# A one-core decoder kernel: the encoder's eight row stores per four batches issued in pairs over two frames

## The reference

```python
x = _layernorm(x + attention_block(x))       # 16 heads; its own two layer norms and a ReLU feed-forward inside
x = _layernorm(x + cross_attention(x, ctx))  # 16 heads, a band of +-64 positions; call the result x3
gout = x3 @ Wg.T                             # x3 as 4096 rows, 8 experts
topv, topi = top_k(gout, 2)                  # each row goes to two experts
out = sum over the two of w * expert(x3)     # gated feed-forward of width 256
```

## Time and profile before

| | us |
|---|---|
| median of 3 runs | 1834.86 |
| the profiled execution, its own time | 1833.47 |
| its span, first to last instruction | 1831.7 |
| TensorE busy | 1330.0 (73%) |
| VectorE busy | 1176.1 (64%) |
| ScalarE busy | 774.5 (42%) |
| GpSimd busy | 543.1 (30%) |
| mean granted TensorE clock | 0.844 |

### The profile page before, as it was taken

One profiled execution on the slowest core, in us unless ns is written; L12 is line 12 of the kernel. 1 busy time (PEld: TensorE's weight loads), 2 busy tenths in 40 slices (PEclk: granted clock), 3 DMA queues, 4 the chain that ended last, 5 costly groups with the idle time before them and its releaser, 6 DMA issues. The chain is left out here.

```text
span 1831.7 us, 34467 instructions
## 1 busy us (share of the span) xinstructions
PE 1330.0 (73%) x10054; PEld 888.8 (49%) x10055; DVE 1176.1 (64%) x3540; ACT 774.5 (42%) x2050; POOL 543.1 (30%) x740
## 2 busy tenths in 40 slices
PE   4788878787878786429995888888577777545950
PEld 2455555455545454315553555555226666544740
DVE  4567768676767675348885898898481111655754
ACT  3677667676767674201221565565321111101210
POOL 1223343434243423220005555553130000341026
PEclk9799999999999998659996999999795555557975
DMA  6000000000000000012215000000100000111123
GB/s 231 14 12 13 17 21 16 24 14 24 13 24 10 18 6 17 20 38 64 64 58 190 20 21 23 20 20 4 29 23 0 0 0 0 42 52 45 56 69 94
DMA packets 83440, 65.44 MB, mean 36 GB/s; under 512 B 12016, under 2 KB 78192, under 8 KB 82416
## 3 DMA queue, kind: packets, MB, share of 16 engines
q1 hardware_dynamic: 71616, 46.06, 8.0%
q0 software_dynamic: 6656, 13.64, 2.3%
q10 hardware_dynamic: 5040, 4.11, 0.7%
HBM read 40.70 MB, written 23.07 MB: 35 GB/s over the span
## 5 line engine op out<-in xcount | busy, mean ns | idle before, releaser
L767 ACT ACTIVATE e_probs<-e_scores,e_neg_max 128x128 f32<-128x128 f32 x512 | 163.8, 400 | 91.8 <-DVE e_neg_max L971 91.7
L586 PE MATMUL e_bank_turned<-c_matrices,e_probs 128*128 128x128 f32 x1024 | 167.4, 288 | 24.6 <-ACT e_probs_t L807 21.3
L530 POOL TENSOR_TENSOR e_rstd<-e_var_eps,c_minus_half 128x1 f32<-128x1 f32 x128 | 70.5, 552 | 360.3 <-DVE e_var_eps L843 360.2
L807 ACT ACTIVATE e_probs_t<-e_bank_turned 128x512 f32<-128x512 f32 x256 | 152.4, 595 | 19.1 <-PE e_bank_turned L586 16.2
L586 PEld LDWEIGHTS e_bank_turned<-c_matrices,e_probs 128*128 128x128 f32 x1024 | 120.1, 147 | 46.0 <-issue 27.7
L763 ACT ACTIVATE e_probs<-e_scores 128x512 f32<-128x512 f32 x128 | 80.7, 630 | 116.0 <-DVE e_scores L968 115.7
L1576 ACT ACTIVATE d_probs<-d_scores 128x512 f32<-128x512 f32 x128 | 81.3, 635 | 112.1 <-DVE d_scores L1615 112.0
L1196 PE MATMUL m_wide<-up,m_rowsT 128*128 x224 | 120.3, 620 | 9.0 <-DVE m_rowsT L1249 7.3
L1793 DVE TENSOR_TENSOR n_gated<-n_gates,states 128x32 f32 x126 | 24.3, 193 | 154.1 <-ACT states L1894 154.1
L596 PE MATMUL e_bank_mix<-e_probs_t,e_values 128*32 128x128 f32 x2048 | 112.7, 293 | 4.0 <-ACT e_probs_t L807 1.3
L1855 PE MATMUL n_pz<-n_gated,n_wa 128*128 128x32 f32 x256 | 80.9, 409 | 45.3 <-DVE n_gated L1793 45.1
(11 more groups left out here) (308 smaller groups left out, 3299.3 us busy)
## 6 DMA issues: line engine op xcount, KB each, us to landing
m_rows<-scratch_sorted SPq DMA_DIRECT2D x112, 64.0 KB, 1.8
scratch_expert_out<-m_y SPq DMA_DIRECT2D x112, 64.0 KB, 1.6
e_x_in<-in_x SPq DMA_DIRECT2D x32, 64.0 KB, 1.9
e_ctx_in<-in_ctx SPq DMA_DIRECT2D x32, 64.0 KB, 2.0
up<-in_m_wgv SPq DMA_DIRECT2D x1, 2048.0 KB
up_b<-in_m_bgv SPq DMA_DIRECT2D x1, 2048.0 KB
scratch_ctxT<-e_xT_ctxT SPq DMA_DIRECT2D x32, 64.0 KB, 1.5
scratch_x<-e_x SPq DMA_DIRECT2D x32, 64.0 KB, 1.5
```

The costliest lines, as they stand in the source:

```text
L586: last = nc.tensor.transpose(turned_bank[:, j * P:(j + 1) * P], pr[k % 3][:, j, :], c["ident"][:])
L767: last = nc.scalar.activation(pr[k % 3][:, j, :], sc[k % 4][:, j, :], ACT.Exp, bias=nmax[k % 4][:, j:j + 1], scale=1.0)
L807: nc.scalar.activation(pt[k % 2][:], turned_bank[:], ACT.Copy).then_inc(probs_t_ready, 1)
```

## The change

In the encoder's GpSimd program the single call `pool_scatter` at offset 71 is replaced by four pieces, at offsets 75, 77, 83 and 85 (places 3 and 5 of the next frame, and 3 and 5 of the one after). Each issues the two stores of one of the four tiles; the first waits for the row numbers as before. `pool_scattered` goes from offset 80 to 94 (place 6 of the frame of the last pair). Within a tick the pieces stay in the order of the code, so they come behind the other GpSimd steps of their tick. The list of ticks is made 16 longer, so that the last group's steps are still within it.

```diff
-ENCODE_TICKS = range(-10, FRAME * (BATCH + SHIFT) + 48)
+ENCODE_TICKS = range(-10, FRAME * (BATCH + SHIFT) + 64)
...
-                if (n := group_at(tick, 71)) is not None:
-                    pool_scatter(nc, pool, r, c, n // SLOTS, [x3[(n - 3 + s) % 10] for s in range(SLOTS)], scr["sorted0"])
-                if (n := group_at(tick, 80)) is not None:
+                for s in range(SLOTS):
+                    if (n := group_at(tick, (75, 77, 83, 85)[s])) is not None:
+                        if s == 0:
+                            pool.wait_ge(r["rows_ready"], LEAD + n // SLOTS + 1)
+                            stand_alone(pool, c)
+                        for q in range(2):
+                            nc.gpsimd.indirect_dma_start(
+                                out=scr["sorted0"], out_offset=bass.IndirectOffsetOnAxis(ap=r["row_u"][:, s, q:q + 1], axis=0),
+                                in_=x3[(n - 3 + s) % 10][:], in_offset=None).then_inc(r["scattered"][s], 16)
+                if (n := group_at(tick, 94)) is not None:
                     pool_scattered(pool, r, n // SLOTS)
```

## The result

| | before | after |
|---|---|---|
| median, same chip | 1833.59 (1832.14 to 1838.01, 4 runs) | 1786.46 (1785.12 to 1790.21, 4 runs) |
| profiled execution, its own time | 1833.47 | 1786.06 |
| its span | 1831.7 | 1784.3 |
| mean granted TensorE clock | 0.844 | 0.862 |

The ratio is 0.9742 with the interval [0.9719, 0.9766], some 47 us faster. The forecast was 1784. Both programs have the same number of instructions. In what follows lines after the changed function have moved by seven: 987 is now 994, 933 is 940, 843 is 850, 911 is 918, 1007 is 1014; the stores are line 580.

What follows compares the result with a forecast made beforehand. Bound: in encoder frames with stores, VectorE and then TensorE wait for GpSimd's power steps behind eight stores. 36.1 + 6.5 + 6.7 = 49.3 us off 1833.47 gives 1784.2, forecast 1784 (chance 0.80); range 1777 to 1801.

Steps and rivals of the forecast that it cites:

- The stop goes, and nothing is late next: Five full encoder frames with stores become 20.11 us frames, since `placed` is hidden in a TensorE wait; 36.1 us saved.
- Sixth row: Stores at n = 23, running into attention-1-only frames: TensorE's 5.58 us gap plus about 1 us of lower clock; 6.5 saved.
- Seventh row: Stores at n = 27, from 750.54: TensorE's 6.69 us wait for x3 goes; 6.7 us saved.
- Pairs at place 3: Offsets 75 and 83, between `x2_bo` and `power(0)`: 2.8 us used of 6.0 idle on GpSimd; hidden, 3.2 to spare.
- Pairs at place 5: Offsets 77 and 85, between `by_place(1)` and `x1_b2`: `x1_b2` 1.2 us late, `power(1)` on time; cost 0.
- part of the new pairs shows: Rival: each pair at place 5 costs its 1.2 us, 17 us back in all, 1801 us; chance 0.08.
- The release: `pool_scattered` at offset 94, nine ticks behind the last pair, finds its semaphores full; cost 0.
- The tail: At the encoder's end the last two pairs land before the last `row_u` needs release, 0.8 us to spare; otherwise 2 lost.
- The shared port: Rival: VectorE and GpSimd lock shared SBUF ports, pairs hold VectorE operations; 27 us back, 1811 us; chance 0.04.
- The signs: Expected in the trace: line 987's wait gone, 20.1 us frames, no early 4 us TensorE gap, clock near 1.0.
- the stop is replaced: Rival: TensorE or the release would hold line 987 as long as GpSimd did; no change, 1833 us; chance 0.03.
- the pairs lie on the path: Rival: GpSimd steps behind each pair set the frame, 11 us per group for 7.2 lost; 1861 us; chance 0.05.

Runs made afterwards that it cites:

- warm_stop: Kernel before with its eight-store stops, twenty extra matmuls filling TensorE's gap in six of them; 1825.28 us, ratio 0.9929.
- fours_place3: Changed kernel with four stores at offset 75 and four at 83, both place 3; 1790.83 us, ratio 0.9779.
- one_block_place3_b: Changed kernel with all eight stores in one piece at offset 75 (place 3), repeated on the third chip; 1804.58 us, ratio 0.9813.
- fours_75_77: Changed kernel with four stores at offset 75 (place 3) and four at 77 (place 5), in one frame; 1788.86 us, ratio 0.9732.
- release_only: Kernel before, eight stores still at offset 71, only pool_scattered moved from 80 to 94 and the tick list lengthened; 1837.32 us, ratio 0.9988.
- fours_71_75_b: Changed kernel with four stores at offset 71 (place 7) and four at 75 (place 3), repeated on the third chip; 1793.69 us, ratio 0.9758.
- one_block_place5: Changed kernel with all eight stores in one piece at offset 77 (place 5); 1826.73 us, ratio 0.997.
- fours_71_75: Changed kernel with four stores at offset 71 (place 7) and four at 75 (place 3), on the first chip; 1803.7 us, ratio 0.9806.
- one_block_place3: Changed kernel with all eight stores in one piece at offset 75 (place 3), on the first chip; 1823.8 us, ratio 0.9916.

## Why the prediction was right

Point by point, by its own steps:

- **The stop goes, and nothing is late next.** Right. All frames from 243.15 to 589.13 are 20.1 to 20.2 us but the four with `picked` (21.0 to 21.4). 345.98 us against 381.54: 35.6 saved, 36.1 predicted. What is missing are two frames of 20.2 and one with `picked` of 21.4, where I had counted 20.11 and 21.0; the kernel before has frames of 20.19 and 21.34 too.
- **Sixth row.** From the fifth stop's end to the `power(1)` behind the sixth row: 710.06 - 620.86 = 89.20 before, 672.05 - 589.13 = 82.92 after. 6.3 saved, 6.5 predicted. The sum was right, its parts hardly: I wrote a gap of 5.6 and 1 us of clock, and `warm_stop` passes the same stretch in 87.14 us, so about 2.1 of it is the clock and 4.2 the wait. That the two errors cancel is luck.
- **Seventh row.** From the moment at which VectorE has written the variance for `power(3)` of batch 30 to the start of that of batch 31: 766.31 - 751.75 = 14.56 before, 721.53 - 713.58 = 7.95 after. 6.6 saved, 6.7 predicted. The 4 us that I took for it at the lower end of the range stand nowhere in the working.
- **Eighth row.** 0 predicted. 35.6 + 6.3 + 6.6 = 48.5 of the 48.4 us between the two ends, so nothing is left for it.
- **Pairs at place 3.** 3.2 us to spare predicted, 3.11 left. That it is slack and not chance shows where it is used up: four stores there cost nothing in the frames (`fours_place3`), eight cost 1.4 to 2.9 us in two frames (`one_block_place3_b`), where 10.1 us of issues go into 6.0 us of idle time and 2.2 come out as a wait.
- **Pairs at place 5.** `x1_b2` 1.2 us late predicted, 0.9 measured; `power(1)` on time. The rival *part of the new pairs shows* is out by those frames, and `fours_75_77` shows that even twice the piece stays hidden but for 0.2 us.
- **The release.** Cost 0: by `release_only`, ratio 0.9988.
- **The tail.** The seventh group's last store ends at 727.18 and `row_u` is written at 729.45, behind a wait of 0.17 us for VectorE's own `keep_rows`; the release does not hold it. I had put 2.0 us between the two points; it is 2.3.
- **The shared port.** The rule of the Trainium skill (SBUF — State Buffer, in "SBUF: two separate sides") that I set against the rows of the stores took no time here either: beside the second pair line 975 takes 0.67 us, within its usual 0.63 to 0.69, and the stores keep their 0.96. I had put the rule too widely: the page says that descriptors starve beside VectorE's modes that use both ports, not beside every operation with two inputs, and line 933, on whose row I leaned, has two inputs. The trace has a nearer test in the very operation that is stretched elsewhere, line 994 at 714.25 and 722.13 of the changed kernel: a store starts 0.2 us before each of them ends, and they take 0.35 us, as against 0.34 at 700.43 with no store beside. What agrees with the lock are VectorE's operations beside GpSimd's arithmetic: line 994 takes 1.57 or 1.58 us where it runs beside `power(2)` and `by_place` (in the kernels with a stop at place 7 and in `fours_71_75_b`), 0.69 beside `by_place` alone in an ordinary frame, and 0.35 in the last frames; that GpSimd's operation is the cause was not tried by itself. Nor does the stretch cost time: `fours_71_75_b` has it with frames of 20.1 us, and `warm_stop` has it with frames only as long as the wait makes them. So the 6.97 us that I explained by line 987 and the clock are the wait and the clock.
- **The signs.** VectorE's wait, the frames, TensorE's gaps (none above 2.3 us between us 60 and 724) and the clock (1.00 over us 100 to 600, 0.97 over 600 to 700) came as written, but not "the first store of the last group at about 768": it is at 730.43. I had taken only the seventh row's 6.7 us off the old 775.01 and forgotten the 42.6 of the six rows before it.
- **The window of the earlier trace rows.** It is not all behind the gap. The clock falls while TensorE is idle, and the gap ends only at 259.78; the low clock that costs time is the 4.60 us from 259.70 on.

So one term was mis-sized, and hidden in a measured sum: in the forecast of the five frames I took 6.97 and 7.2 us from the trace and needed no split. Only where I split the clock's 2.3 us stood as 1 us (the sixth row and `warm_stop`) or was left out (`one_block_place5`). In the sixth row the error cancelled, the frames of `one_block_place5` came out dearer, and `warm_stop` gained more than I wrote.

The rivals *the stop is replaced* and *the pairs lie on the path* are out by the 20.11 us frames. The second one's mechanism is real, though: with eight stores at place 5 a step behind them is late, and most of the gain is gone.

## What to carry to other kernels

A row of short issues on an in-order queue costs what its last follower is late, not what it takes itself: write down for each gap of that engine how long it is and when somebody reads what comes next, and cut the row into pieces that fit. Here the four cuts tried, all into pieces of at most 5 us, kept the gain, and where the pieces lay hardly mattered; only on the first chip, with its late results, did the one that ran there (`fours_71_75`) keep less. And price a stop of TensorE as the wait plus the low clock behind it, which here was almost half as much again.

## What the runs showed of the hardware

Results that came late, on one chip. In the traces of all four kernels on the first chip VectorE or ScalarE waits for a TensorE result that TensorE's own records show as done earlier, by 2.8 us in the rows below and by up to 4.4 (`release_only`); the trace pairs such a wait with nothing and says "remote". It always stands beside a row of four or more stores, or within 3 us behind it. From `one_block_place3` the timelines of TensorE and VectorE, and the row of its wait table, us 240 to 650:

```profile
262.00 0.60 PE L696 MATMUL e_bank_vec<-c_matrices,e_mix_t 128*128 128x128 f32 x4
...
265.45 0.26 DVE L859 RECIPROCAL e_rsum<-e_bank_vec 128x16 f32<-128x16 f32 x1 [4.02 <-remote]
...
DVE e_rsum L859 <- remote: 15.8, 4, 4.0
```

`release_only`, whose stores stand where the kernel before has them, shows it too (waits of ScalarE, us 240 to 650), but under its own stop, where it costs nothing to be seen:

```profile
ACT e_probs_t L807 <- remote: 16.3, 5, 4.1
```

No trace of the changed kernel, of the kernel before, or of any kernel on the second and third chip has one such wait, the repeated `one_block_place3` and `fours_71_75` among them. By size they account for the difference of the twins, 0.9916 against 0.9813 and 0.9806 against 0.9758: the five pairs of frames of `one_block_place3` are 19 us longer in the trace on the first chip, and 1.0% of the time is 19 us. Whether small pieces are also the sturdier choice is not shown, since the changed kernel did not run on that chip. What delays the results there is open: I have no run that changes it, and can't say whether it is the chip or the hour.

The other surprise is how short a gap of TensorE can be enough. In `one_block_place3_b` TensorE has one in each of the five frames with stores, ahead of the same line:

```profile
273.31 1.14 PE L625 MATMUL e_bank_scores<-e_k_by_place,e_q_k_k 32*128 32x512 f32 x8 [1.97 <-DVE e_scores L975]
...
356.61 1.14 PE L625 MATMUL e_bank_scores<-e_k_by_place,e_q_k_k 32*128 32x512 f32 x8 [1.69 <-DVE e_scores L975]
```

Within about 1 us of the end of the gap of 1.97 us the clock fell to its lower level for some 3 us, and so it did at two gaps of 1.68 us (that end at 522.25 and 605.68). At two of 1.69 and 1.67 us (356.61 and 439.45) it stayed at 1.00. The three pairs of frames in which it fell took 42.46, 41.97 and 43.11 us, the other two 41.61 and 41.80. So gaps of one length, in one place, went either way, and their length alone doesn't foretell the clock.
